# A vision tower on one Trainium2 core: attention's output products, its last division and one split, in another order

## The chip, the cores and the metric

The kernel runs on one core of one Trainium2 chip. Five engines work side by side, each through its own list of instructions in order: TensorE (PE, with its weight loads as PEld) multiplies and transposes, VectorE (DVE) and ScalarE (ACT) do elementwise work and read what TensorE left in PSUM, GpSimd (POOL) works in SBUF alone, and SyncE (SP) issues DMAs. They meet through semaphores only: an instruction that waits holds up everything behind it on its engine. The metric is the device time of one execution in microseconds (us), as the median of several.

## What is computed

One block of a vision transformer over 16 images of 37 positions (a class token and 36 patches), 592 rows of width 192. Cut to what matters:

```
h = patches of x, layer-normed over 3840 values, times W (3840x192), + b
h = concat(cls_tok, h)                                # 16 x 37 x 192
h = h + attention(layernorm(h))                       # 12 heads of 16, softmax with a bias by distance
h = h + ffn(layernorm(h))                             # shared expert (768) and 8 experts (192), two chosen

attention: q, k, v = x @ w_q.T + b_q, ...
           ctx  = softmax(q k / 4 + bias) @ v
           return ctx @ w_o.T + b_o
```

## The kernel before

The 592 rows lie in five tiles of 128 (tile 4 is part full), and the 16 images in eight pairs p of 74 rows. Large products in f16 are made of a high and a low part of each operand: ACT rounds a matrix to f16 (the high part) and DVE subtracts that from the original (the low part). No scheduler orders the work. Each engine's order is the order in which its calls are written, and semaphores named by the engine that raises them (p_, a_, v_, g_) tie them together.

The change lies in the stretch between the attention scores and the first feed-forward products. For its last pairs this happens:

- `scores(u)` on PE (L670, L680) makes the scores of two pairs, `differences(u)` on DVE (L1442, L1446) subtracts the row's largest, `exps(u)` on ACT (L1047) takes the exponential, `pt(p)` on PE (L695) transposes a pair, `weights_copy(p)` on ACT (L1072) copies it from PSUM, and `av(p)` on PE (L714) multiplies it with the values.
- `normalise(i)` on DVE (L1455, L1457) divides the contexts of pairs 2i and 2i+1 by their sums, `ct(p)` on PE (L729, L730) transposes them, and `ctx_high(i)` on ACT (L1066, eight small copies for the first two calls, four each) brings them back to SBUF as CA and CC.
- `wo(t)` on PE (L740, L742) is the output product of tile t. It waits until ACT has copied all pairs that reach into the tile: `ctx_high(0)` for tile 0, up to `ctx_high(3)` for tiles 3 and 4.
- `add_attention(t)` on DVE (L1478) adds the product to the residual stream in h2, L1374 and L1382 take mean and variance, `variances(k)` ends with L1385, `root(k)` on ACT (L985) takes the root, `rsqrt(k)` on DVE (L1334 to L1341) finishes it, `normed` (L1392) writes the normed tile, and `transposes(1, ...)` on PE (L600, L602) turns it. `copies` (L1003) on ACT comes between the two transposes of a tile. The tiles go in two groups: 0 to 2, then 3 and 4.
- `high_parts(1, ...)` on ACT (L996, L997) and `low_parts(1, ...)` on DVE (L1402) split the turned tiles, and `gu(i)` on PE (L828) multiplies them with the feed-forward weights. `gu(0)` and `gu(1)` run interleaved: twelve matmuls that need only the high parts, then eight that need the low parts. `gu(1)` waits for all five additions. Behind them come the transposes of tiles 3 and 4.
- The weights of the first third of the feed-forward are split in the same stretch: `ffn_high(0, q)` on ACT (L979) and `ffn_low(0, q)` on DVE (L1314), six steps each, wherever they are written in.

ACT changes its function table twice here, to Sqrt (L1088) and to Silu (L1095). PSUM has eight banks. SP's loads of the next weights wait for the last `av` and the last split (L386).

Of the kernel before, what the change touches and what calls it, by code (L numbers as in the profile page):

```python
# [20 lines left out]
ALU = mybir.AluOpType  # L21
# [3 lines left out]
P = 128  # L25
IMAGES, POSITIONS, D = 16, 37, 192
N = IMAGES * POSITIONS
# [70 lines left out]
def vit_kernel(nc, x_inner, x_ring, w_inner, w_ring, gb, consts, j_rev, ind, tok_b, cls, tab,  # L98
               aw_a, aw_b, aw_c, f_a, f_b, f_d, gate_rows, out):
    with ExitStack() as ctx:  # L100
# [176 lines left out]

        def attention_out(t):

            c0 = D * (0, 1, 0, 0, 1)[t]  # L280
            return PS[:, (3, 3, 4, 5, 5)[t], c0:c0 + D]

        def lane_cols(w, g):

# [141 lines left out]
        def _(pe):  # L426
# [167 lines left out]
            def transposes(n, banks, tiles):  # L594

                for t in tiles:
                    pe.wait_ge(S["v_hn"], TILES * n + t + 1)
                    oa = PS[:, banks[0], t * P:(t + 1) * P] if t < 3 else PS[:, banks[2], (t - 3) * P:(t - 2) * P]
                    ob = PS[:, banks[1], t * P:(t + 1) * P] if t < 3 else PS[:, banks[2], (t - 1) * P:t * P]
                    nc.tensor.transpose(oa, hn[:, t, 0:P], ident)  # L600
                    pe.wait_ge(S["a_dup"], TILES * n + t + 1)
                    nc.tensor.transpose(ob, hn[:, t, P:2 * P], ident).then_inc(S["p_t"], 1)  # L602
# [97 lines left out]
            def av(p):  # L700

                pe.wait_ge(S["a_pth"], p + 1)
                pe.wait_ge(d_vr[p // 4], 96)
                if p == 0:
                    pe.wait_ge(S["a_q"], 4)
                if p == 2:
                    pe.wait_ge(S["a_v"], 5)
                if p in (4, 6):
                    pe.wait_ge(S["v_cn"], p - 2)
                for r in range(LANES):  # L710
                    for bi in (0, 1):
                        q0, q1 = (0, 64) if bi == 0 else (64, QROWS)
                        c0 = (p % 2) * LANES * VW + r * VW
                        last = mm(PS[q0:q1, 1 + p // 2 % 2, c0:c0 + VW], PT[:, p, r, q0:q1],  # L714
                                  vv[:, 2 * p + bi, :, r * HV:(r + 1) * HV],
                                  start=(p % 2 == 0 and r == 0), stop=True, skip_group_check=True)
                last.then_inc(S["p_av"], 1)

            def ct(p):

                pe.wait_ge(S["v_cn"], p + 1)
                pe.wait_ge(S["g_one"], 2)
                if p == 0:
                    pe.wait_ge(S["v_sub"], 4)
                if p == 6:
                    pe.wait_ge(S["a_pth"], PAIRS)
                b = context_bank(p // 2)
                c0 = (p % 2) * 2 * QROWS
                nc.tensor.transpose(PS[:, b, c0:c0 + QROWS], cn[:, p, 0:P], ident[0:QROWS, 0:QROWS])  # L729
                nc.tensor.transpose(PS[:, b, c0 + QROWS:c0 + 2 * QROWS], cn[:, p, P:2 * P],  # L730
                                    ident[0:QROWS, 0:QROWS]).then_inc(S["p_ct"], 1)

            def wo(t):

                need = min(2 * (t + 1), PAIRS)
                pe.wait_ge(S["a_chi"], need)
                if t == 4:
                    pe.wait_ge(S["g_rows"], 2)
                tok = slice(t * P, (t + 1) * P)
                mm(attention_out(t), CA[:, tok], awst[:, 0, OC:OC + D], start=(t in (0, 2, 3)), stop=False,  # L740
                   skip_group_check=True)
                last = mm(attention_out(t), CC[:, tok], awst[0:CROWS, 2, OC:OC + D], start=False, stop=True,  # L742
                          skip_group_check=True)
                last.then_inc(S["p_wo"], 1)
# [34 lines left out]
                av(p)  # L779
            for p in (6, 7):  # L780
                pt(p)
            for p in range(4):
                ct(p)
            for p in (6, 7):
                av(p)
            for p in (4, 5):
                ct(p)
            for t in range(3):
                wo(t)
            for p in (6, 7):  # L790
                ct(p)
            wo(3)
            wo(4)
            transposes(1, (0, 1, 2), range(3))

            def router():

# [86 lines left out]
        def _(act):  # L884
# [86 lines left out]
            def ffn_high(p, q):  # L971

                if q == 0:
                    act.wait_ge(d_f[p], 48)
                Ah, _, Bw, Dh, _ = split(p)
                k, m = divmod(q, 2)
                W, st = (Ah, Bw, Dh)[k], stages(p)[k]
                part = slice(3 * m, 3 * m + 3) if k == 2 else slice(m, m + 1)
                A(W[:, part], st[:, part], ACT.Copy, scale=SW).then_inc(S["a_fw"], 1)  # L979

            def root(k):

                row, tiles, ready = NORMS[k]
                act.wait_ge(S["v_stat"], ready)
                A(small[:, row + 1, tiles[0]:tiles[-1] + 1], small[:, row, tiles[0]:tiles[-1] + 1],  # L985
                  ACT.Sqrt).then_inc(S["a_sqrt"], 1)
# [18 lines left out]
            def kq_high(f):  # L1005

                q, g, half = kq_product(f)
                cols = slice(half * HALF, (half + 1) * HALF)
                act.wait_ge(S["p_q" if q else "p_k"], 2 * half + g + 1)
                if f == 0:  # L1010
                    act.wait_ge(S["v_kk"], 2)
                if q:
                    A(Q32[:, g, cols], PS[:, kq_bank(f), 0:HALF], ACT.Copy, scale=QKS / XW).then_inc(S["a_q"], 1)
                else:
                    A(K32[:, 0, cols], PS[:, kq_bank(f), 0:HALF], ACT.Copy, scale=keven[:, :])
                    A(K32[:, 1, cols], PS[:, kq_bank(f), 0:HALF], ACT.Copy, scale=kodd[:, :]).then_inc(S["a_k"], 1)
# [36 lines left out]
            kq_high(6)  # L1053
            ffn_high(0, 1)
            kq_high(7)
            for t in (3, 4, 5):
                values_copy(t)
            exps(1)
            ffn_high(0, 2)

            def ctx_high(i):

                act.wait_ge(S["p_ct"], 2 * i + 2)
                for k, (C, rows) in enumerate(((CA, P), (CC, CROWS))):
                    for pr in (0, 1):
                        last = A(pair_cols(C, 2 * i + pr, rows), pair_queries(context_bank(i), pr, k, rows), ACT.Copy)  # L1066
                last.then_inc(S["a_chi"], 2)

            def weights_copy(p):

                act.wait_ge(S["p_pt"], p + 1)
                A(PT[:, p].rearrange("p r q -> p (r q)"), PS[0:BLOCK, (0, 7)[p % 2], 0:LANES * QROWS],  # L1072
                  ACT.Copy).then_inc(S["a_pth"], 1)
# [7 lines left out]
                weights_copy(p)  # L1081
            exps(3)
            ffn_high(0, 5)
            for p in (6, 7):
                weights_copy(p)
            ctx_high(0)
            ctx_high(1)
            A(small[:, 46, 0:1], one[:, :], ACT.Sqrt)  # L1088
            ctx_high(2)
            ctx_high(3)  # L1090
            root(3)
            copies(1, range(3))
            high_parts(1, (0, 1, 2), 0)
            root(4)
# [125 lines left out]
        def _(dve):  # L1220
# [86 lines left out]
            def ffn_low(p, q):  # L1307
# [6 lines left out]
                V.scalar_tensor_tensor(out=W[r0:P, part], in0=st[r0:P, part], scalar=SW, in1=hi[r0:P, part],  # L1314
                                       op0=ALU.mult, op1=ALU.subtract).then_inc(S["v_fw"], 1)

            for k in range(3):
                queries_keys_low(k)

# [47 lines left out]
            def residual(n, op, tiles):  # L1367

                src = (h1, h2)[n]
                for t in tiles:  # L1370
                    op(t).then_inc(S["v_h"], 1)
                for t in tiles:
                    dve.wait_ge(S["v_h"], TILES * n + t + 1)
                    V.bn_stats(bst[:, t, :], src[:, t, :]).then_inc(S["v_bn"], 1)  # L1374
                    bn[0] += 1
# [89 lines left out]
            ffn_low(0, 0)  # L1465
            differences(1)
            ffn_low(0, 1)
            differences(2)
            normalise(0)
            differences(3)  # L1470
            ffn_low(0, 2)
            normalise(1)
            normalise(2)
            for q in (3, 4):
                ffn_low(0, q)
            def add_attention(t):
                dve.wait_ge(S["p_wo"], (2, 2, 3, 5, 5)[t])
                return V.scalar_tensor_tensor(  # L1478
                    out=h2[:, t, :], in0=attention_out(t),
                    scalar=1.0, in1=h1[:, t, :], op0=ALU.mult, op1=ALU.add)  # L1480

            normalise(3)
            ffn_low(0, 5)
            residual(1, add_attention, (0, 1))
            residual(1, add_attention, (2,))
            variances(3)
            V.memset(ah[:, :, N:NPAD], 0.0)
            V.memset(al[:, :, N:NPAD], 0.0).then_inc(S["v_pad"], 1)
            rsqrt(3)
            dve.wait_ge(S["p_t"], TILES)  # L1490
            normed(1, range(3))
            residual(1, add_attention, (3, 4))
            variances(4)
            low_parts(1, (0, 1, 2), 0)
            rsqrt(4)
# [230 lines left out]
```

## Time and profile before

| what | us |
|---|---|
| median of 3 runs | 147.86 |
| lowest, highest | 147.77, 148.08 |
| the profiled execution, its own time | 147.91 |
| span of the profiled execution | 145.9 |
| PE busy in the span | 134.5 (92%) |
| DVE busy | 105.1 (72%) |
| ACT busy | 86.2 (59%) |
| POOL busy | 50.9 (35%) |
| share of PE in the chain that ended last | 64% |
| share of DVE, of ACT | 14%, 8% |

The profiled execution's own time is 2.0 us more than its span, which begins and ends with the engines' first and last work. Busy shares are averages over stages with different limits: in the stretch of this change three engines hand work to one another, so its rows are read one by one. "Idle before <-releaser" in brackets tells how long an engine stood before an instruction and what ended that. Rows of one engine overlap a little, since the next instruction starts while the last one drains.

### The profile page before, as it was taken

Reading aid. Unit: us, or ns where it says so; the run is one execution under the profiler, and the core shown is the slowest. Engines: PE = TensorE matmul, PEld = TensorE weight load, DVE = VectorE, ACT = ScalarE, POOL = GpSimd, SP = SyncE. Lnnn points to the kernel's source line nnn. Section 1 sums busy time; section 2 is a strip of 40 time slices with the busy share of each in tenths; the row PEclk is TensorE's granted clock in tenths of the full one; section 3 lists DMA queues with packets and bytes.
Section 4 is the critical chain, followed back from the end, with each engine's and each line's share of the span. In section 5 each row is a group of like instructions: output and inputs, shape, how many; then the busy total and the mean of one; then the engine's idle time right before and its main releaser. Section 6 shows DMA issues by size and latency. Waiting matters only on the chain.

```text
span 145.9 us, 3999 instructions
## 1 busy us (share of the span) xinstructions
PE 134.5 (92%) x1556; PEld 105.6 (72%) x1556; DVE 105.1 (72%) x268; ACT 86.2 (59%) x206; POOL 50.9 (35%) x72
## 2 busy tenths in 40 slices
PE   7768999999999999997899999998999999999991
PEld 2327679884676787985578788886887888888890
DVE  5499996899977978899876999838666224224453
ACT  0668769640488887883889756566553344344430
POOL 8149000500000000000025334785777577477330
PEclk9999999999999999999999999999999999999998
DMA  4999993078002233007993000368980000000003
GB/s 120 399 366 391 317 344 59 0 233 360 0 7 66 50 92 71 0 4 242 393 404 154 0 0 10 96 181 229 257 231 13 0 4 0 0 0 4 2 0 125
DMA packets 10580, 19.05 MB, mean 131 GB/s; under 512 B 2886, under 2 KB 6290, under 8 KB 10562
## 3 DMA queue, kind: packets, MB, share of 16 engines
q1 hardware_dynamic: 10218, 18.48, 39.3%
q10 hardware_dynamic: 344, 0.32, 0.8%
q8 instruction: 12, 0.20, 0.6%
q14 instruction: 6, 0.05, 0.1%
HBM read 17.84 MB, written 0.96 MB: 129 GB/s over the span
## 4 chain that ended last, share of the span: by engine, by line
PE 64%; DVE 14%; ACT 8%; DMA 5%; issue 4%; POOL 2%; SPq 1%; DVEq 0%; POOLq 0%
PE PS L828 25%; PE PS L858 12%; DMA xs<-in_x_inner_dram 5%; DVE we L1265 4%; PE PS L587 4%; PE PS L626 3%; PE PS L714 3%; PE PS L680 2%; PE PS L695 2%; DVE vhl L1579 2%; DVE xhl L1243 2%; POOL vhl L1200 2%; PE PS L670 1%; PE PS L506 1%; PE PS L569 1%
## 5 line engine op out<-in xcount | busy, mean ns | idle before, releaser
L1209 POOL TENSOR_TENSOR kq<-vhl,kq 128x296 f16<-128x296 f32 x35 | 28.2, 806 | 65.7 <-ACT kq L1116 65.7
L1579 DVE SCALAR_TENSOR_TENSOR vhl<-PS,vhl 128x296 f32<-128x296 f32 x36 | 16.8, 465 | 21.1 <-POOL vhl L1200 13.7
L1109 ACT ACTIVATE vhl<-PS 128x296 f32<-128x296 f32 x36 | 15.0, 415 | 25.6 <-PE PS L828 25.5
L1116 ACT ACTIVATE kq<-vhl 128x296 f16<-128x296 f32 x36 | 16.0, 445 | 4.2 <-DVE vhl L1579 4.2
L1200 POOL TENSOR_TENSOR vhl<-vhl,xs 128x296 f32<-128x296 f32 x14 | 12.5, 895 | 6.8 <-issue 6.0
L828 PE MATMUL PS<-XAh,slab 128*128 128x296 f16 x48 | 10.0, 290 | 0.7 <-DVE vhl L1579 0.7
L828 PE MATMUL PS<-XAh,piece 128*128 128x296 f16 x48 | 9.5, 289 | 1.0 <-ACT XAh L996 0.7
L1265 DVE SCALAR_TENSOR_TENSOR we<-slab,gbs,we 128x192 f32<-128x192 f32 x24 | 9.0, 445 | 1.6 <-ACT we L917 1.6
L828 PE MATMUL PS<-XAh,xsq 128*128 128x296 f16 x48 | 10.0, 289 | 0.0
L506 PE MATMUL PS<-whl,xhl 128*128 128x192 f16 (+1 forms) x40 | 9.9, 247 | 0.0
L508 PE MATMUL PS<-whl,xhl 128*128 128x192 f16 (+1 forms) x40 | 9.9, 246 | 0.0
L509 PE MATMUL PS<-whl,xhl 128*128 128x192 f16 (+1 forms) x40 | 9.8, 245 | 0.0
L858 PE MATMUL PS<-piece,kq 128*128 128x192 f16 x90 | 8.4, 246 | 0.0
L858 PE MATMUL PS<-slab,kq 128*128 128x192 f16 x90 | 8.4, 246 | 0.0
L858 PE MATMUL PS<-xsq,kq 128*128 128x192 f16 x90 | 8.2, 246 | 0.1
L858 PEld LDWEIGHTS PS<-xsq,kq 128*128 128x128 f16 x90 | 7.5, 98 | 0.5 <-issue 0.3
L858 PEld LDWEIGHTS PS<-slab,kq 128*128 128x128 f16 x90 | 7.6, 98 | 0.3
L858 PEld LDWEIGHTS PS<-piece,kq 128*128 128x128 f16 x90 | 7.6, 98 | 0.3
L492 PE MATMUL PS<-oneh 128*128 128x512 f16 x20 | 6.7, 498 | 1.0 <-DVE oneh L1223 1.0
L828 PE MATMUL PS<-XB,slab 128*128 128x296 f16 x24 | 6.9, 289 | 0.0
L828 PE MATMUL PS<-XAl,slab 128*128 128x296 f16 x24 | 6.9, 289 | 0.0
L828 PE MATMUL PS<-wring,slab 128*128 128x296 f16 x24 | 6.9, 289 | 0.0
(242 smaller groups left out, 363.9 us busy)
## 6 DMA issues: line engine op xcount, KB each, us to landing
slab<-in_w_inner_dram SPq DMA_DIRECT2D x3, 960.0 KB, 9.0
xs<-gate_rows_dram SPq DMA_DIRECT2D x8, 296.0 KB, 8.2
xs<-in_x_inner_dram SPq DMA_DIRECT2D x3, 592.0 KB, 10.0
stage<-in_f_a_dram SPq DMA_DIRECT2D x2, 768.0 KB, 4.9
stage<-in_f_b_dram SPq DMA_DIRECT2D x2, 768.0 KB, 6.4
stage<-gate_rows_dram SPq DMA_DIRECT2D x8, 148.0 KB, 7.3
stage<-in_f_d_dram SPq DMA_DIRECT2D x2, 576.0 KB, 7.1
xhl<-in_f_a_dram SPq DMA_DIRECT2D x1, 768.0 KB, 8.6
```

What stands on the lines that cost most here:

```text
L492: mm(PS[:, 1, :], oneh[:, :].to_broadcast([P, P]), oneh[:, :].to_broadcast([P, 512]), start=True, stop=True)
L506: mm(patch_out(t), xh[0:K, j, tok], wh[0:K, j, 0:D], start=(j == 0 and t in (0, 2, 3)), stop=False, skip_group_check=True)
L508: mm(patch_out(t), xl[0:K, j, tok], wh[0:K, j, 0:D], start=False, stop=False, skip_group_check=True)
L509: return mm(patch_out(t), xh[0:K, j, tok], wl[0:K, j, :], start=False, stop=(j == CHUNKS - 1), skip_group_check=True)
L828: last = mm(gate_up(i, m), w5[m][k], x5[k], start=(k == 0), stop=(k == 4))
L858: last = mm(o, a[:, f % ABUF, tok], w[:, f % PT_, :], start=(f in (0, ST) and t % 2 == 0 and k == 0), stop=(f in (ST - 1, FT - 1) and k == ...
L1109: A(silu[:, i % 2, :], gate_up(i, 0), ACT.Silu, scale=1.0 / XW).then_inc(S["a_silu"], 1)
L1116: A(ah[:, f % ABUF, half * HALF:(half + 1) * HALF], hf[:, i % 3, :], ACT.Copy).then_inc(S["a_ah"], 1)
L1200: G.tensor_tensor(sgate[:, i % 2, :], silu[:, i % 2, :], Gb[:, f_expert(f)[0], cols], ALU.mult).then_inc(S["g_sg"], 1)
L1209: G.tensor_tensor(al[:, f % ABUF, cols], hf[:, i % 3, :], ah[:, f % ABUF, cols], ALU.subtract).then_inc(S["g_al"], 1)
L1265: V.scalar_tensor_tensor(out=we[:, j, :], in0=slabv[:, s, j, :], scalar=gbs[:, 0, s * INNER + j:s * INNER + j + 1], in1=we[:, j, :], op0=A ...
L1579: V.scalar_tensor_tensor(out=hf[:, i % 3, :], in0=gate_up(i, 1), scalar=SH / XW, in1=src[:, i % 2, :], op0=ALU.mult, op1=ALU.mult).then_in ...
```

## The change

Four edits, all in the order of work or the place of results:

1. The product of tile 1 gets bank 6 and that of tile 4 bank 7, where they lay beside tiles 0 and 3 in banks 3 and 5. Each addition waits for its own product alone, and each tile is added and measured before the next.
2. PE makes the products of tiles 0, 1 and 2 before `av(6)` and `av(7)`, and turns tiles 0 to 2 between the products of tiles 3 and 4. ACT copies the contexts of pairs 0 to 5 between the weights of pair 6 and those of pair 7, and takes `root(3)` ahead of `ctx_high(3)`.
3. DVE makes the last division, `normalise(3)`, behind `variances(3)` and before `rsqrt(3)`. The two fills of the padding go behind the normed tiles.
4. DVE's third split step (64x768) becomes two of 64x384, ahead of `differences(2)` and behind `normalise(0)`. ACT's step for it moves up by four places, and DVE's other steps each move up by one place.

```diff
         def attention_out(t):
-            c0 = D * (0, 1, 0, 0, 1)[t]
-            return PS[:, (3, 3, 4, 5, 5)[t], c0:c0 + D]
+            return PS[:, (3, 6, 4, 5, 7)[t], 0:D]
...
-            for p in range(4):
-                ct(p)
-            for p in (6, 7):
-                av(p)
-            for p in (4, 5):
+            for p in range(6):
                 ct(p)
             for t in range(3):
                 wo(t)
             for p in (6, 7):
+                av(p)
+            for p in (6, 7):
                 ct(p)
             wo(3)
+            transposes(1, (0, 1, 2), range(3))
             wo(4)
-            transposes(1, (0, 1, 2), range(3))
...
+            ffn_high(0, 2)
             for t in (3, 4, 5):
                 values_copy(t)
             exps(1)
-            ffn_high(0, 2)
...
-            for p in (6, 7):
-                weights_copy(p)
-            ctx_high(0)
-            ctx_high(1)
+            weights_copy(6)
+            for i in range(3):
+                ctx_high(i)
+            weights_copy(7)
             A(small[:, 46, 0:1], one[:, :], ACT.Sqrt)
-            ctx_high(2)
+            root(3)
             ctx_high(3)
-            root(3)
...
+            def up_low_half(m, c):
+                _, _, Bw, _, _ = split(0)
+                part = (slice(64, P), m, slice(c * PC // 2, (c + 1) * PC // 2))
+                dve.wait_ge(S["a_fw"], 3 + m)
+                return V.scalar_tensor_tensor(out=Bw[part], in0=stages(0)[1][part], scalar=SW, in1=Bw[part],
+                                              op0=ALU.mult, op1=ALU.subtract)
...
             ffn_low(0, 1)
+            up_low_half(0, 0)
             differences(2)
             normalise(0)
+            up_low_half(0, 1).then_inc(S["v_fw"], 1)
             differences(3)
-            ffn_low(0, 2)
+            ffn_low(0, 3)
             normalise(1)
             normalise(2)
-            for q in (3, 4):
+            for q in (4, 5):
                 ffn_low(0, q)
             def add_attention(t):
-                dve.wait_ge(S["p_wo"], (2, 2, 3, 5, 5)[t])
+                dve.wait_ge(S["p_wo"], t + 1)
...
+            for t in range(3):
+                residual(1, add_attention, (t,))
+            variances(3)
             normalise(3)
-            ffn_low(0, 5)
-            residual(1, add_attention, (0, 1))
-            residual(1, add_attention, (2,))
-            variances(3)
-            V.memset(ah[:, :, N:NPAD], 0.0)
-            V.memset(al[:, :, N:NPAD], 0.0).then_inc(S["v_pad"], 1)
             rsqrt(3)
             dve.wait_ge(S["p_t"], TILES)
             normed(1, range(3))
-            residual(1, add_attention, (3, 4))
+            V.memset(ah[:, :, N:NPAD], 0.0)
+            V.memset(al[:, :, N:NPAD], 0.0).then_inc(S["v_pad"], 1)
+            for t in (3, 4):
+                residual(1, add_attention, (t,))
             variances(4)
```

In the kernel after, lines from 281 on have moved by one to six. On PE the end of attention stood so before, from the product of tile 2 (`we` holds the copied contexts, `xs` the divided ones, `hn` the normed tiles):

```order
L740 MATMUL PS<-awst,we 128x192 [waits a_chi]
L742 MATMUL PS<-awst,we 128x192
L729 MATMUL PS<-cst,xs 128x101 [waits a_pth,g_one,v_cn]
L730 MATMUL PS<-cst,xs 128x101
L729 MATMUL PS<-cst,xs 128x101 [waits g_one,v_cn]
L730 MATMUL PS<-cst,xs 128x101
L740 MATMUL PS<-awst,we 128x192 [waits a_chi]
L742 MATMUL PS<-awst,we 128x192
L740 MATMUL PS<-awst,we 128x192 [waits g_rows,a_chi]
L742 MATMUL PS<-awst,we 128x192
L600 MATMUL PS<-cst,hn 128x128 [waits v_hn]
```

The same end of attention on PE now, from the last transposes of the contexts (`av(6)` and `av(7)` stand right in front of those):

```order
L729 MATMUL PS<-cst,xs 128x101
L739 MATMUL PS<-awst,we 128x192 [waits a_chi]
L741 MATMUL PS<-awst,we 128x192
L599 MATMUL PS<-cst,hn 128x128 [waits v_hn]
L601 MATMUL PS<-cst,hn 128x128 [waits a_dup]
L599 MATMUL PS<-cst,hn 128x128 [waits v_hn]
L601 MATMUL PS<-cst,hn 128x128 [waits a_dup]
L599 MATMUL PS<-cst,hn 128x128 [waits v_hn]
L601 MATMUL PS<-cst,hn 128x128 [waits a_dup]
L739 MATMUL PS<-awst,we 128x192 [waits g_rows,a_chi]
L741 MATMUL PS<-awst,we 128x192
```

The first three tiles are turned behind one product instead of two, and the product of tile 4 comes after them. On DVE the last division stood so before, ahead of the additions (`rden`, `xs`: the division; `h`: the residual stream):

```order
L1455 RECIPROCAL rden<-PS 101x24 [waits p_av]
L1457 TENSOR_TENSOR xs<-PS,rden 101x2x192 [waits v_rd]
L1314 SCALAR_TENSOR_TENSOR piece<-stage,piece 128x576 [waits a_fw]
L1478 SCALAR_TENSOR_TENSOR h<-PS,h 128x192 [waits p_wo] x2
L1374 BN_STATS bst<-h 128x6 [waits v_h] x2
L1478 SCALAR_TENSOR_TENSOR h<-PS,h 128x192 [waits p_wo]
L1374 BN_STATS bst<-h 128x6 [waits v_h]
L1382 BN_AGGR mv<-bst 128x2 [waits v_bn]
L1382 BN_AGGR mv<-bst 128x2 x2
L1385 TENSOR_SCALAR small<-mv 128x3 [waits v_bn]
```

And on DVE now, from the addition of tile 2:

```order
L1484 SCALAR_TENSOR_TENSOR h<-PS,h 128x192 [waits p_wo]
L1378 BN_STATS bst<-h 128x6 [waits v_h]
L1386 BN_AGGR mv<-bst 128x2 [waits v_bn]
L1386 BN_AGGR mv<-bst 128x2 x2
L1389 TENSOR_SCALAR small<-mv 128x3 [waits v_bn]
L1459 RECIPROCAL rden<-PS 101x24 [waits p_av,v_stat]
L1461 TENSOR_TENSOR xs<-PS,rden 101x2x192 [waits v_rd]
L1338 RECIPROCAL small<-small 128x3 [waits a_sqrt]
L1343 TENSOR_TENSOR small<-small 128x3 [waits v_stat]
```

The division has gone behind the three additions and the variance, and it now waits for that variance (v_stat) as well as for `av(7)`.

## Rows read from the trace of the kernel before

**Rows 1.** The chain that ended last: start us, length us, what.

```profile
44.17 0.11 PE PS L600
...
70.82 2.68 PE PS L828 x20
```

**Rows 2.** Timeline of ACT, 61 to 67: start, length, engine, line, tiles, [idle before].

```profile
61.11 0.91 ACT L1072 ACTIVATE xhl<-PS 111x404 f32<-111x404 f32 x2 [0.65 <-PE PS L695]
61.90 1.09 ACT L1066 ACTIVATE we<-PS 128x74 f32<-128x74 f32 x8
63.01 1.28 ACT L1088 ACT_TABLE_LOAD   x1
...
64.41 0.58 ACT L1066 ACTIVATE we<-PS 128x74 f32<-128x74 f32 x4
66.35 0.60 ACT L1066 ACTIVATE we<-PS 128x74 f32<-128x74 f32 x4 [1.36 <-PE PS L730]
```

**Rows 3.** Timeline of PE, 61 to 66.

```profile
61.30 0.25 PE L729 MATMUL PS<-cst,xs 101*128 101x101 f32 x1
...
61.90 0.25 PE L730 MATMUL PS<-cst,xs 101*128 101x101 f32 x1
62.08 1.14 PE L714 MATMUL PS<-vhl,xhl 111*64 111x51 f32 x32
...
63.55 0.51 PE L740 MATMUL PS<-awst,we 128*128 128x192 f32 x2
...
64.23 0.49 PE L740 MATMUL PS<-awst,we 128*128 128x192 f32 x2
...
65.81 0.25 PE L729 MATMUL PS<-cst,xs 101*128 101x101 f32 x1
```

**Rows 4.** Timeline of DVE, 63 to 68.

```profile
63.27 0.31 DVE L1455 RECIPROCAL rden<-PS 101x24 f32<-101x24 f32 x1
63.68 0.56 DVE L1457 TENSOR_TENSOR xs<-PS,rden 101x384 f32<-101x384 f32 x1
...
65.08 0.62 DVE L1478 SCALAR_TENSOR_TENSOR h<-PS,h 128x192 f32<-128x192 f32 x2 [0.17 <-PE PS L742]
...
66.15 0.34 DVE L1478 SCALAR_TENSOR_TENSOR h<-PS,h 128x192 f32<-128x192 f32 x1
...
67.27 0.17 DVE L1385 TENSOR_SCALAR small<-mv 128x3 f32<-128x3 f32 x1
```

**Rows 5.** Timeline of all engines, 67 to 71: root, normed tiles, last transpose, high part.

```profile
67.71 0.18 DVE L1334 RECIPROCAL small<-small 128x3 f32<-128x3 f32 x1
...
68.51 0.96 DVE L1392 TENSOR_SCALAR hn<-h,mv,small 128x192 f32<-128x192 f32 x3
...
69.82 0.33 PE L602 MATMUL PS<-cst,hn 128*128 128x128 f32 x1
...
70.18 0.49 ACT L996 ACTIVATE XAh<-PS 128x384 f16<-128x384 f32 x1 [0.42 <-PE PS L602]
```

**Rows 6.** The same timeline, 71 to 74: tiles 3 and 4 on DVE and PE.

```profile
71.30 0.56 DVE L1402 SCALAR_TENSOR_TENSOR XAl<-PS,XAh 128x384 f16<-128x384 f32 x1 [0.28 <-ACT XB L997]
...
72.23 0.14 DVE L1334 RECIPROCAL small<-small 128x2 f32<-128x2 f32 x1
...
73.44 0.14 PEld L600 LDWEIGHTS PS<-cst,hn 128*128 128x128 f32 x1 [0.26 <-DVE hn L1392]
```

**Rows 7.** Timeline of DVE, 42 to 57: a split of half size, two idle times.

```profile
42.06 0.57 DVE L1304 SCALAR_TENSOR_TENSOR WB<-awst,WB 64x393 f16<-64x393 f32 x1
...
52.59 1.08 DVE L1442 TENSOR_REDUCE mx<-PS 101x24 f32<-101x888 f32 x1 [0.70 <-PE PS L680]
...
56.30 1.08 DVE L1442 TENSOR_REDUCE mx<-PS 101x24 f32<-101x888 f32 x1 [0.43 <-PE PS L680]
```

**Rows 8.** Timeline of all engines at 58.5 and of PE at 83.

```profile
58.53 0.95 DVE L1314 SCALAR_TENSOR_TENSOR piece<-stage,piece 64x768 f16<-64x768 f32 x1
...
82.96 0.43 PE L828 MATMUL PS<-XAh,piece 128*128 128x296 f16 x2 [0.33 <-DVE vhl L1579]
```

More of the change, by code:

```diff
@@ L739, in wo @@
                 tok = slice(t * P, (t + 1) * P)
-                mm(attention_out(t), CA[:, tok], awst[:, 0, OC:OC + D], start=(t in (0, 2, 3)), stop=False,
+                mm(attention_out(t), CA[:, tok], awst[:, 0, OC:OC + D], start=True, stop=False,
                    skip_group_check=True)
```

## The prediction, made before the change was timed

> **What bounds the kernel now.** I read the chain that ended last first, since it tells which stage sets the end. From 57 to 74 us it runs through this stretch without a break, and from 70.82 on it is TensorE alone with the twenty matmuls of the first two feed-forward halves, 0.134 us each [rows 1]. So what counts is when TensorE gets to those, and when it gets past the transposes of tiles 3 and 4 behind them. Then I read the engines' timelines from 61 us, where each hand-over shows. ScalarE copies the last two pairs' weights, pays a Sqrt table of 1.28 us in the middle of the contexts, and waits 1.36 us for TensorE before the last context [rows 2]. TensorE makes the last two value products early, from 62.08 to 63.22, and then the output products, 0.68 us each where nothing waits [rows 3]. VectorE divides at once, at 63.27, and is ready for the additions at 65.08 [rows 4]. The root and the normed tiles follow at 67.71 and 68.51, the last of the six transposes at 69.82, the high part at 70.18 [rows 5]. Tiles 3 and 4 are turned at 73.44, after 0.26 us of waiting for VectorE [rows 6]. All the work behind that hangs on what it hands over.
>
> **The split in two halves: nothing.** A whole step takes 0.95 us [rows 8]. A half of 64x384 is bounded by half of that, 0.48, and by a step of 64x393, 0.57 [rows 7]. I take 0.55, being nearer to the row of that width. The first half falls into 0.70 us of idle time. The second falls into 0.43 us, so it may delay the last score maxima by 0.05 to 0.14 [rows 7]. ScalarE, whose exponential would wait for that, is busy with weight copies then, which covers it. The two halves take 0.95 us of VectorE out of the later stretch. ScalarE's cast moves ahead of the value copies and delays those by about 0.3; their readers come over 1 us later. If that cover were gone, 0.14 us at most would be lost on VectorE's side and 0.3 on ScalarE's.
>
> **Products ahead of the last value products: earlier additions.** The transposes start at 61.30 and follow at 0.086, each 0.25 long [rows 3], so the first context is ready at 61.81 and ScalarE, now one weight copy shorter, starts on it at 61.84. Four copies take 0.60 alone, 0.48 in a row [rows 2]: the first context ends at 62.44, the third at 63.40. From the end of a context's copies at 64.99 [rows 2] to TensorE's next work behind the product it released, 65.81 [rows 3], are 0.82. So product 1 starts at 62.44 + 0.82 = 63.26, product 2 at 63.94, and TensorE is free for the value products at 64.62. From a product's start (64.23 [rows 3]) to its addition (65.08 [rows 4]) are 0.85: the addition of tile 2 starts at 63.94 + 0.85 = 64.79 instead of 66.15. From there to the end of the variance's chain are 1.12 (66.15 to 67.27 [rows 4]): 65.91 instead of 67.27, a gain of 1.36. The own banks cost nothing and let tile 0's addition go ahead of product 1; tile 2's sets the end, so this gives nothing either.
>
> **The Sqrt table: covered.** The seventh weight copy ends at 63.8, the table of 1.28 [rows 2] at 65.1, the root starts at 66.1.
> Here the Trainium skill speaks against the change (ScalarE: Activation LUTs, What ACT_TABLE_LOAD costs): a switch is about 1283 ns and a drain of 1380 ns behind it. The trace agrees with the first and shows no drain, since 64.41 follows on 63.01 + 1.28 with a dummy activation between [rows 2]. With the drain the Sqrt switch would still fit before the root, but the later Silu switch, which now starts 0.7 later, would hold the first silu by a further 1.4 us.
>
> **The last division: 1 us behind what the output needs.** The value products end at 64.62 + 1.14 = 65.76. The division stands behind the variance: 65.91, 0.17 long [rows 4], and 0.10 to the next step as between the division's own two, so 66.18. Its second part starts 0.41 later and takes 0.56 [rows 4]: 67.15, where it was 64.24. VectorE's own chain loses little by this: the root ran meanwhile, and its reciprocal starts at 67.1 instead of 67.71, the normed tiles at 67.9 instead of 68.51 [rows 5]. But TensorE's order decides. Four transposes take 0.57 out of a wait (three steps of 0.086, 0.25, 0.06 to get going), from 67.21 to 67.78. The last context's copies start at 67.81 and end at 68.41 [rows 2]. Product 3 waits for them and the transposes of the normed tiles stand behind it: 68.41 + 0.82 = 69.23. With all tiles ready these go at 0.11 [rows 1], the last at 69.78 instead of 69.82 [rows 5]. So 1.36 us of gain have shrunk to 0.04, and the first feed-forward matmul starts at 70.78 instead of 70.82.
>
> **Product 4 behind the transposes: the loss.** It starts at 69.89 and its addition at 69.89 + 0.85 = 70.74. VectorE has been done with everything else since 69.0 and waits. From this addition to the end of the variance I take 1.02 (1.12 less about 0.1 for two tiles in place of three): 71.76. The low parts stand behind that, + 0.27 as above: 72.03 instead of 71.30 [rows 6]. From there on the order is as before: 0.93 to the reciprocal [rows 6], 0.80 to the normed tiles [rows 5], 0.41 to TensorE: 74.17 instead of 73.44. TensorE will have finished all twenty matmuls by then but for a wait for the low parts, which cover 70.78 to 73.46. **The sum is + 0.73 us at TensorE's transposes of tiles 3 and 4.** Root 4 and the Silu table behind it move by as much, so nothing catches up there. SP's loads of the next weights wait for the value products and start up to 0.8 later; they have no reader for some 8 us, so that costs nothing.
>
> The profiled execution took 147.91, so + 0.73 is 148.64. The median of the runs stands 0.05 below that execution: **148.6**.
>
> **Rivals.** *Partly taken up (no change).* If the division started when the value products end, at 65.8, the tail would be 0.4 shorter, + 0.35; and a later wait of 0.33 [rows 8] could take the rest, if it isn't moved along. For it: VectorE's hand-overs are my least sure terms. Against: the row at 82.96 is a wait for VectorE, whose chain starts from the moved work. It gives 147.9. *Faster.* The addition of tile 4 would have to be early enough for both the low parts (by 72.2) and the normed tiles (by 73.4) to be ready when TensorE asks. Then the 0.26 of waiting [rows 6] and up to 0.2 at the front are won: 147.4. It decides at a last context ready by 67.6, against 68.41 above. For it: the variance is 1.36 earlier, and each of the seven hand-overs is only an estimate. Against: the value products alone, at 65.76, leave 0.4 of the 0.8. *More than forecast.* TensorE stands idle for 1.4 us from 65.8 and 0.6 from 67.8. Before, its granted clock stayed at 2.4 GHz through waits of up to 0.7. A fall to 1.2 GHz would double the twenty matmuls' 2.68 us [rows 1]: some 151.
>
> **How the numbers follow.** Forecast (148.2 to 149.0) 0.67; no change 0.16; faster 0.11; more than forecast 0.06. A measurement of this kernel can tell about 0.2%, 0.3 us, from no change. Faster by more than that has 0.11, slower by more 0.67 + 0.06 = 0.73. The range has to reach to the no-change case: 147.8 to 149.0 leaves out some 0.17.
>
> **What would show it.** In the profile after: the addition of tile 2 near 64.8 and its variance near 65.9; the division near 66.2, right behind the variance; a wait of TensorE of about 1.4 us before the last context's transposes, and one of 0.6 before product 3; the transposes of the normed tiles behind product 3 without a wait for VectorE; a wait of VectorE of over 1 us before the addition of tile 4; the low parts near 72.0 and TensorE's transposes of tiles 3 and 4 near 74.2; and from there on every step 0.7 later than before. It is wrong if the division runs before the variance, if product 3 is done before the normed tiles are, or if waits behind 80 us shrink by what was lost.

## The result, and the profile after the change

The changed kernel took 149.18 us (median of 4 executions, 148.43 to 150.37) against 147.81 before: a ratio of 1.0087, 95% interval 1.0055 to 1.0119. It is slower, as forecast, but by 1.37 us instead of 0.7, and the median lies above the range. Here and below a ratio leaves out executions over 1.5% above the fastest of their kernel and the medians leave out none, so that a ratio stands below the quotient of its medians where long executions are many.

The four times can't be understood without TensorE's mean granted clock: 148.43 (0.998), 148.57 (0.999), 149.78 (0.988) and 150.37 (0.984). Two of them kept the full clock nearly throughout, two didn't. The profiled one is of the first kind, 148.43 against 147.91 before, + 0.52. I take that first, and then what the other kind adds.

PE, from the last value products on, in the timeline after the change (start, length, engine, line, tiles, [idle before <-releaser]; lines stand one to six off those of before):

```profile
64.55 1.13 PE L713 MATMUL PS<-vhl,xhl 111*64 111x51 f32 x32
67.03 0.30 PE L728 MATMUL PS<-cst,xs 101*128 101x101 f32 x1 [1.34 <-DVE xs L1461]
...
68.28 0.59 PE L739 MATMUL PS<-awst,we 128*128 128x192 f32 x2 [0.69 <-ACT we L1063]
...
69.04 0.27 PE L599 MATMUL PS<-cst,hn 128*128 128x128 f32 x1
...
69.69 0.49 PE L739 MATMUL PS<-awst,we 128*128 128x192 f32 x2
...
70.53 0.66 PE L825 MATMUL PS<-XAh,piece 128*128 128x296 f16 x4
...
72.44 0.42 PE L825 MATMUL PS<-XAl,piece 128*128 128x296 f16 x2 [0.24 <-DVE XAl L1406]
...
73.97 0.33 PE L599 MATMUL PS<-cst,hn 128*128 128x128 f32 x1
...
83.48 0.43 PE L825 MATMUL PS<-XAh,piece 128*128 128x296 f16 x2 [0.33 <-DVE vhl L1585]
```

These answer to [rows 3], [rows 5] and [rows 6]. One wait is new, 1.34 us for the last division. The 0.69 for the last context was there before, at 67.00:

```profile
67.00 0.59 PE L740 MATMUL PS<-awst,we 128*128 128x192 f32 x2 [0.69 <-ACT we L1066]
```

It now comes 1.28 us later, and starts 0.56 us behind the end of the new one. The waits of 0.37 and 0.67 us that the kernel before had behind its product 4, for the normed tiles and for the high part, are gone in exchange. The transposes of tiles 0 to 2 (69.04) stand right behind product 3, waiting for nothing. Those of tiles 3 and 4 start at 73.97 instead of 73.44, and the wait at 83.48 is 0.33 long as it was at 82.96 [rows 8]: the loss is carried on unchanged.

DVE in the same timeline, which answers to [rows 4] and [rows 6]:

```profile
64.68 0.34 DVE L1484 SCALAR_TENSOR_TENSOR h<-PS,h 128x192 f32<-128x192 f32 x1
...
65.80 0.17 DVE L1389 TENSOR_SCALAR small<-mv 128x3 f32<-128x3 f32 x1
66.00 0.31 DVE L1459 RECIPROCAL rden<-PS 101x24 f32<-101x24 f32 x1
66.41 0.56 DVE L1461 TENSOR_TENSOR xs<-PS,rden 101x384 f32<-101x384 f32 x1
66.89 0.17 DVE L1338 RECIPROCAL small<-small 128x3 f32<-128x3 f32 x1
...
67.68 0.96 DVE L1396 TENSOR_SCALAR hn<-h,mv,small 128x192 f32<-128x192 f32 x3
...
70.55 0.36 DVE L1484 SCALAR_TENSOR_TENSOR h<-PS,h 128x192 f32<-128x192 f32 x1 [0.56 <-PE PS L741]
...
71.82 0.56 DVE L1406 SCALAR_TENSOR_TENSOR XAl<-PS,XAh 128x384 f16<-128x384 f32 x1
...
73.53 0.67 DVE L1396 TENSOR_SCALAR hn<-h,mv,small 128x192 f32<-128x192 f32 x2
```

The variance is 1.47 us earlier than in [rows 4] (65.80 for 67.27), the normed tiles 0.83 earlier than in [rows 5] (67.68 for 68.51), and yet the low parts come 0.52 later than in [rows 6] (71.82 for 71.30).

### The profile page after: what moved, and what is told of

Read it like the earlier page. It is cut to its first block, busy times and chain, and to the rows that moved or that the text cites. A ratio compares the mean times of both kernels' runs of the same rounds, so it can differ in the third digit from the quotient of the medians.

```text
span 146.4 us, 4001 instructions
## 1 busy us (share of the span) xinstructions
PE 134.9 (92%) x1556; PEld 105.6 (72%) x1556; DVE 105.6 (72%) x269; ACT 85.9 (59%) x206; POOL 50.9 (35%) x72
## 4 chain that ended last, share of the span: by engine, by line
PE 62%; DVE 16%; ACT 8%; DMA 5%; issue 4%; POOL 2%; SPq 1%; DVEq 0%; POOLq 0%
PE PS L825 23%; PE PS L855 12%; DMA xs<-in_x_inner_dram 5%; DVE we L1261 4%; PE PS L586 4%; PE PS L625 3%; PE PS L679 2%; PE PS L713 2%; PE PS L694 2%; DVE vhl L1585 2%; DVE xhl L1239 2%; POOL vhl L1196 2%; PE PS L669 1%; PE PS L505 1%; PE PS L568 1%
```

## The experiments

The theory from the prediction: the division behind the variance makes the last context late, product 3 and the transposes queue behind it, and product 4 behind those makes the tail late. New beside it: in some executions TensorE's granted clock falls in this stretch. The rivals: the spread has nothing to do with the stretch; the banks or the halves cost the time. All ran with 8 to 12 executions, beside 23 to 35 of the kernel before, whose medians were 147.96, 147.97 and 147.98. They ran in three groups, each on a chip of its own. The first had the changed kernel again, the long wait filled, product 4 moved alone and the early division; the second the short wait filled, the halves, the whole split and the banks; the third product 4 moved with the long wait filled, and the early division again. So the changed kernel ran beside the first group only. Three single executions took over 300 us (341.55, 341.51, and 466.74 of the kernel before); they stand in the medians and not in the counts. Without them the early division has 147.57 instead of 147.62, and the whole split 147.84 instead of 147.87.

**The changed kernel again.**

> The changed kernel once more, to see how its times are spread. Four executions gave 148.43, 148.57, 149.78 and 150.37 us, with a mean granted clock of 0.998, 0.999, 0.988 and 0.984. Theory A (the clock falls in some executions): again two groups, one at 148.4 to 148.7 with a clock of 0.998 or more, one 1 to 2 us longer with a clock under 0.99, some half of them. Theory B (chance of the session, as in any kernel): nearly all at 148.4 to 148.7, or the kernel before beside it is spread as well.

Measured: 149.85 us, ratio 1.0099 (1.0067 to 1.0132). Two of eight executions took 148.52 and 148.93 at a clock of 0.998 and more, six 149.64 to 150.85 at 0.986 to 0.988. With the four above that is 4 against 8. The quotient of the medians is 1.013; the ratio leaves out the longest execution. The lowest clock among the 31 executions of the kernel before beside it was 0.996. It isn't quite proof against a fall either: of all 89 executions of the kernel before in the three groups one took 149.41 us at a clock of 0.988. Theory A holds, and this profiled execution is of the long kind. Its stretches, with TensorE's granted clock in the column PEclk (1.00 is 2.4 GHz, 0.50 is 1.2 GHz):

```profile
core 0: us, PE busy (x) PEld busy (x) DVE busy (x) ACT busy (x) POOL busy (x), PEclk, DMA share, GB/s
66.00:68.00 2.00, 0.66 (x16) 0.54 (x13) 1.76 (x9) 0.20 (x1) 0.00 (x0) 1.00 0.09 11
68.00:70.00 2.00, 1.31 (x8) 1.10 (x7) 1.46 (x8) 1.25 (x7) 0.00 (x0) 0.88 0.91 296
70.00:72.00 2.00, 2.00 (x10) 1.93 (x9) 0.72 (x2) 0.40 (x2) 0.00 (x0) 0.50 0.98 361
72.00:74.00 2.00, 2.00 (x13) 1.51 (x13) 1.02 (x5) 0.47 (x2) 0.00 (x0) 0.77 1.05 405
```

TensorE was busy for 0.66 and 1.31 of two 2 us stretches, and then its clock was at the lower level throughout the next. The execution above, which stands 0.77 us earlier, was much the same there at the full clock:

```profile
66.00:68.00 2.00, 0.56 (x4) 0.37 (x4) 1.76 (x8) 0.57 (x5) 0.00 (x0) 1.00 0.43 65
68.00:70.00 2.00, 1.72 (x12) 1.70 (x13) 1.52 (x7) 0.99 (x6) 0.00 (x0) 1.00 0.95 341
```

So what TensorE did doesn't settle by itself whether the clock falls. PE's timeline of the long execution:

```profile
65.32 1.14 PE L713 MATMUL PS<-vhl,xhl 111*64 111x51 f32 x32
67.79 0.31 PE L728 MATMUL PS<-cst,xs 101*128 101x101 f32 x1 [1.34 <-DVE xs L1461]
...
69.05 0.59 PE L739 MATMUL PS<-awst,we 128*128 128x192 f32 x2 [0.69 <-ACT we L1063]
69.48 0.80 PE L741 MATMUL PS<-awst,we 97*128 97x192 f32 x2
70.07 0.42 PE L599 MATMUL PS<-cst,hn 128*128 128x128 f32 x1
...
71.35 0.85 PE L739 MATMUL PS<-awst,we 128*128 128x192 f32 x2
71.99 0.85 PE L741 MATMUL PS<-awst,we 97*128 97x192 f32 x2
72.63 0.81 PE L825 MATMUL PS<-XAh,piece 128*128 128x296 f16 x4
...
76.30 0.33 PE L599 MATMUL PS<-cst,hn 128*128 128x128 f32 x1
```

Both waits are as long as above. The clock falls at 69.5, within product 3 (the first pair of its matmuls takes 0.59, the second 0.80), and is back at 72.9, within the first feed-forward matmuls. Product 4 takes 1.28 us from start to the next work, against 2 x 0.33 for its two pairs of matmuls at the full clock (69.69 to 70.02 above). This execution stands 0.77 later than the one above before the stretch begins (65.32 for 64.55), so at the transposes of tiles 3 and 4 the lower clock has cost 76.30 - 73.97 - 0.77 = 1.56 us.

**The long wait filled.** The edit:

```diff
             for p in (6, 7):
                 av(p)
+            keep_warm(1, 6)
             for p in (6, 7):
                 ct(p)
```

> The changed kernel with six dummy matmuls of 512 columns (0.22 us each) on TensorE between the last value product and the last context's transposes, where it waits 1.34 us. They lie inside the wait, so the order of the rest is untouched. Theory A (TensorE's idle time before the last context is what makes the clock fall): all executions at 148.4 to 148.7, clock 0.998 or more. Theory A2 (the other idle times do it as well): long executions are fewer but there. Theory B (the spread has nothing to do with this wait): the same spread as the changed kernel's, median 149.2.

Measured: 148.57 us, ratio 1.0031 (1.0014 to 1.0049). None of twelve executions fell under a clock of 0.995, and the longest took 148.93. PE's timeline:

```profile
65.60 1.47 PE L586 MATMUL PS<-WAh 128*128 128x512 f16 x6
67.00 0.31 PE L728 MATMUL PS<-cst,xs 101*128 101x101 f32 x1
...
73.94 0.33 PE L599 MATMUL PS<-cst,hn 128*128 128x128 f32 x1
```

The work behind starts when it did (73.94 for 73.97). So this separates the two losses: 148.57 - 147.96 = 0.6 us from the order of the work, and the rest from the clock. Six matmuls without use win back 1.3 us of the median of the run beside it, in which the clock was low in six of eight executions.

**The short wait filled.** `keep_warm(1, 3)` stands ahead of `wo(3)` instead, and the long wait stays idle.

> The changed kernel with three dummy matmuls of 512 columns on TensorE in the other wait, the 0.69 us between the last context's transposes and product 3; the 1.34 us before those transposes stay idle. If any idle time of the stretch counts alike, filling half as much makes long executions rarer but not gone (between 1 and 6 in 12, against 8 in 12 of the changed kernel and none in 12 with the longer wait filled). If only the one longest wait counts, they are as frequent as in the changed kernel. Undisturbed executions at 148.4 to 148.7 either way.

Measured: 148.57 us, ratio 1.0036 (1.0014 to 1.0057), none of twelve executions under 0.995. I had expected fewer falls, not none.

```profile
67.20 0.31 PE L728 MATMUL PS<-cst,xs 101*128 101x101 f32 x1 [1.34 <-DVE xs L1462]
...
67.61 0.81 PE L586 MATMUL PS<-WAh 128*128 128x512 f16 x3
68.45 0.59 PE L739 MATMUL PS<-awst,we 128*128 128x192 f32 x2
```

The wait of 1.34 us is still there. Neither wait alone brought the clock down in a dozen executions; the two together went with a low clock in eight of twelve. The changed kernel didn't run in this group, so that this count is compared with one from other chips; for the long wait the two ran side by side.

**Product 4 ahead of the transposes**, first alone, then with the long wait filled as above:

```diff
             wo(3)
-            transposes(1, (0, 1, 2), range(3))
             wo(4)
+            transposes(1, (0, 1, 2), range(3))
```

> The changed kernel with the product of tile 4 back ahead of the transposes of tiles 0 to 2. If the late context alone sets the tail: the transposes start some 0.65 later, near 69.7, tile 4's addition some 0.6 earlier, and the transposes of tiles 3 and 4 start within 0.2 of where they are after the change (73.97): the undisturbed executions at 148.3 to 148.6. If the product's place behind the transposes is the loss, as the prediction has it: the transposes of tiles 3 and 4 come 0.5 earlier, 147.9.

> The changed kernel with product 4 ahead of the transposes of tiles 0 to 2, and the first wait filled with the six dummy matmuls, so that the clock can't blur the comparison with e1_warm (148.57, 12 executions). If the late context alone sets the tail, the undisturbed e3_wo4_first (148.40) was no accident: 148.3 to 148.5, all executions at a clock of 0.995 or more; the transposes of tiles 0 to 2 start some 0.65 later than in e1_warm (69.01) and those of tiles 3 and 4 within 0.25 of 73.94. If the product's place was the loss: 147.9 to 148.1.

Measured: 149.45 us for the first, six executions at 148.16 to 148.93 (median 148.40) and six at 149.97 to 151.32 with a clock of 0.972 to 0.987. The profiled one took 150.89:

```profile
68.35 1.01 PE L739 MATMUL PS<-awst,we 128*128 128x192 f32 x2 [0.69 <-ACT we L1063]
```

Here the clock fell earlier, at 67.9 and within the wait of 0.69 us, and it was low until 74.8, into the feed-forward matmuls. That execution is 2.5 us over the undisturbed median. The second: 148.22 us, ratio 1.0017 (0.9997 to 1.0038), 0.35 below e1_warm, which is between the two outcomes that I had written down. One of its executions had a mean clock of 0.988, at 148.78; it is the profiled one, and its clock fell at 6 to 8 us, under the loads at the start, where TensorE had waited 2.17 us for a DMA, and stood at 1.00 throughout this stretch. So a mean clock of 0.988 alone doesn't tell where the clock fell. Its PE timeline:

```profile
68.93 0.59 PE L739 MATMUL PS<-awst,we 128*128 128x192 f32 x2 [0.69 <-ACT we L1064]
...
70.34 0.27 PE L599 MATMUL PS<-cst,hn 128*128 128x128 f32 x1
...
71.83 0.66 PE L826 MATMUL PS<-XAh,piece 128*128 128x296 f16 x4 [0.67 <-ACT XAh L994]
...
74.35 0.27 PE L599 MATMUL PS<-cst,hn 128*128 128x128 f32 x1
```

Counted from product 3, the transposes of tiles 3 and 4 come at + 5.42 here and at 73.97 - 68.28 = + 5.69 in the changed kernel: 0.27 earlier, though the feed-forward starts 0.65 later. So the product's place was worth 0.35 of the 0.6 by the medians with the wait filled, 0.27 by the trace, and 0.15 by the undisturbed executions of the first run (148.40 against 148.55 of the changed kernel's four, inside what I had written down for the late context alone). What is left goes with the late product 3: the feed-forward can't start before the transposes behind it.

**The last division early.** With banks and halves as changed, but both value products ahead of the output products, the division as soon as they are done, and ScalarE's three contexts ahead of the Sqrt table. Against the changed kernel:

```diff
             for p in range(6):
                 ct(p)
+            for p in (6, 7):
+                av(p)
             for t in range(3):
                 wo(t)
             for p in (6, 7):
-                av(p)
-            for p in (6, 7):
                 ct(p)
             wo(3)
-            transposes(1, (0, 1, 2), range(3))
             wo(4)
+            transposes(1, (0, 1, 2), range(3))
...
             weights_copy(6)
+            weights_copy(7)
             for i in range(3):
                 ctx_high(i)
-            weights_copy(7)
             A(small[:, 46, 0:1], one[:, :], ACT.Sqrt)
-            root(3)
             ctx_high(3)
+            root(3)
...
+            normalise(3)
             for t in range(3):
                 residual(1, add_attention, (t,))
             variances(3)
-            normalise(3)
+            V.memset(ah[:, :, N:NPAD], 0.0)
+            V.memset(al[:, :, N:NPAD], 0.0).then_inc(S["v_pad"], 1)
             rsqrt(3)
             dve.wait_ge(S["p_t"], TILES)
             normed(1, range(3))
-            V.memset(ah[:, :, N:NPAD], 0.0)
-            V.memset(al[:, :, N:NPAD], 0.0).then_inc(S["v_pad"], 1)
-            for t in (3, 4):
-                residual(1, add_attention, (t,))
+            residual(1, add_attention, (3, 4))
```

> Banks of their own, all five transposed pairs up to 5 and both last value products early, the division as soon as they are done, ScalarE's three contexts ahead of the Sqrt table, the output products behind, the product of tile 4 ahead of the transposes, split in two halves. If the late last division is the cause of the loss: additions of tile 2 near 65.6, variance near 66.7, normed tiles near 67.9, and everything behind 0.3 to 0.5 earlier than before: 147.4 (147.2 to 147.6), faster than both. If the own banks or the halves cost something by themselves: 147.8 or more. Clock 0.998 or more in all executions, since no wait of TensorE is longer than before.

> e4_early_ctx once more, to narrow the interval: its first eleven undisturbed executions had a median of 147.57 against 147.96 of the kernel before beside it. If that gain is real: 147.4 to 147.7 again, 0.3 to 0.5 below the kernel before, no execution at a clock under 0.99. If it was chance: 147.8 or more.

Measured: 147.62 us, ratio 0.9975 (0.9955 to 0.9994), and again 147.50, ratio 0.9958 (0.9939 to 0.9976): 0.3 to 0.5 us faster than the kernel before, and the first of the two over 2 us faster than the changed one beside it. No execution fell under a clock of 0.995. From the timeline of all engines:

```profile
63.47 0.31 DVE L1459 RECIPROCAL rden<-PS 101x24 f32<-101x24 f32 x1 [0.73 <-PE PS L713]
...
66.61 0.59 PE L739 MATMUL PS<-awst,we 128*128 128x192 f32 x2 [0.69 <-ACT we L1063]
...
66.79 0.17 DVE L1389 TENSOR_SCALAR small<-mv 128x3 f32<-128x3 f32 x1
...
68.46 0.33 PE L599 MATMUL PS<-cst,hn 128*128 128x128 f32 x1 [0.28 <-DVE hn L1396]
...
72.85 0.27 PE L599 MATMUL PS<-cst,hn 128*128 128x128 f32 x1
```

The variance is a microsecond later than in the changed kernel (66.79 for 65.80), and the kernel is faster: product 3 starts at 66.61 instead of 68.28, so that products 3 and 4 are done when the normed tiles come, and TensorE waits for VectorE again. The transposes of tiles 3 and 4 come at 72.85. This kernel takes back several things at once: product 4 is ahead of the transposes again (0.15 to 0.35 us, as above) and tiles 3 and 4 are added in a pair again. Of the 0.95 us to the changed kernel with its long wait filled (148.57) that leaves some 0.4 to 0.8, an estimate with up to 0.2 for the pairs as measured below, to the early division and what follows from it. The division wasn't moved alone.

**The halves alone, and the halves taken out of the faster kernel.**

> The kernel before with edit 4 alone: the split in two halves in earlier gaps, the other steps one place up. By the prediction it is worth nothing by itself: 147.8 to 148.1, within 0.1% of the kernel before beside it, with the additions of tiles 0 to 2 where they were since they wait for TensorE. The rival, that it lets the last division and the additions start earlier, would give 0.2 us or more.

> The kernel with the early last division (e4) with edit 4 undone. There the division waits 0.73 us for TensorE with the split moved away; with the whole split step of 0.95 us back in front of it, the division should start 0.2 to 0.3 later and the end come later by as much: 147.7 to 147.9 against 147.5. If the halves are worth nothing here either: 147.5.

Measured: 147.77 us, ratio 0.9988 (0.9967 to 1.0008), no difference that this can tell; and for the faster kernel without the halves 147.87, ratio 0.9991 (0.9976 to 1.0005), against 147.50 and 147.62 with them in the other two groups. Without them the division starts at 64.10, right behind the split steps, instead of after a wait of 0.73:

```profile
64.10 0.30 DVE L1459 RECIPROCAL rden<-PS 101x24 f32<-101x24 f32 x1
...
71.43 0.56 DVE L1406 SCALAR_TENSOR_TENSOR XAl<-PS,XAh 128x384 f16<-128x384 f32 x1 [0.28 <-ACT XB L994]
```

The execution above with its 63.47 stands 0.35 earlier from the context transposes on. The second profile with the halves is level with this one (context transposes at 61.48 and 61.50) and has the division at 63.80, 0.3 earlier. So the halves are worth some 0.3 us in that order, by the traces and the medians; the intervals of the ratios overlap or touch.

The second line shows something that I hadn't looked for. In all three kernels without the halves (before, the banks alone, this one) the low parts start 0.44 to 0.46 us behind the start of the variance's last step, with 0.28 idle. With the halves they start 0.20 or 0.21 behind it, in all traces but that of product 4 moved alone, where the high part came late; with the halves alone that is 71.12 instead of 71.30 [rows 6]. The profile names ScalarE's last high part for the wait, but in the kernel before that ends at 71.05, 0.25 ahead of the low parts. Why the halves take this wait away is not shown. The variance's last step in the kernel before, for the 0.46:

```profile
70.84 0.17 DVE L1385 TENSOR_SCALAR small<-mv 128x2 f32<-128x2 f32 x1
```

**The banks and the tile-by-tile order alone.**

> The kernel before with edit 1 alone: products 1 and 4 in banks of their own, each tile added and measured before the next. Tile 2's addition is set by product 2, so the variance stays where it was: within 0.1 us of the kernel before beside it (147.8 to 148.1). If the one-at-a-time order costs VectorE 0.1 us per tile, tiles 3 and 4, which are not covered by TensorE, come 0.1 to 0.2 later: up to 148.1.

Measured: 148.23 us, ratio 1.0014 (0.9997 to 1.0032); eleven executions at 148.06 to 148.35, one at 149.20 with a clock of 0.988. The interval just touches no change. DVE's timeline shows where 0.2 us go (this execution stands 0.07 earlier than that of before, the context transposes at 61.23):

```profile
67.19 0.17 DVE L1384 TENSOR_SCALAR small<-mv 128x3 f32<-128x3 f32 x1
...
69.31 0.35 DVE L1477 SCALAR_TENSOR_TENSOR h<-PS,h 128x192 f32<-128x192 f32 x1
69.69 0.36 DVE L1373 BATCH_NORM_STATS2 bst<-h 128x6 f32<-128x192 f32 x1
69.97 0.34 DVE L1477 SCALAR_TENSOR_TENSOR h<-PS,h 128x192 f32<-128x192 f32 x1
...
71.46 0.56 DVE L1401 SCALAR_TENSOR_TENSOR XAl<-PS,XAh 128x384 f16<-128x384 f32 x1 [0.28 <-DVE small L1384]
```

For tiles 0 to 2 nothing is lost (67.19 for 67.27 [rows 4]). For tiles 3 and 4 a measurement that needs the addition in front of it starts 0.38 us behind it (69.31 to 69.69), and one instruction that needs nothing 0.28 (69.69 to 69.97). Additions and measurements in pairs hide that; one by one they don't, and the low parts start at 71.46 instead of 71.30 [rows 6]. The Trainium skill (VectorE: DVE Perf Modes, The DRAIN you can't avoid) tells of eight copies that took the same time with a semaphore behind each and with one behind the last only. Here every addition and every measurement raises a semaphore, and what costs 0.1 us is to wait for that of the instruction right in front, at a length of 0.35 us; no run here shows it for longer ones.

## Why the prediction was wrong

By its own steps, for an execution whose clock holds, it was right nearly throughout. The trace after stands 0.10 us earlier than that of before by 61 us (the context transposes start at 61.20, not 61.30), so 0.10 of each difference below is this head start.

| step | forecast | measured |
|---|---|---|
| addition of tile 2 | 64.79 | 64.68 |
| end of the variance's chain | 65.91 | 65.80 |
| division | 66.18 | 66.00 |
| last context's transposes | 67.21 | 67.03 |
| transposes of tiles 0 to 2 | 69.23 | 69.04 |
| first feed-forward matmul | 70.78 | 70.53 |
| addition of tile 4 | 70.74 | 70.55 |
| low parts | 72.03 | 71.82 |
| transposes of tiles 3 and 4 | 74.17 | 73.97 |
| profiled execution | 148.64 | 148.43 |

- **The step that failed is the clock's term, which the sum put at nothing.** The two waits of TensorE entered the sum as time only, and every matmul behind them at the full clock. The fall stood in the rival "more than forecast" with a chance of 0.06 and a price of 2.7 us, and the range ended at 149.0 without it. Measured: 8 of 12 executions ran at a mean clock of 0.984 to 0.988 and took 149.64 to 150.85 instead of 148.43 to 148.93, and with the long wait filled none of twelve did. The argument for the low chance, that the clock had held through waits of up to 0.7, spoke of a stretch without a wait of 1.34 followed by one of 0.69; for the two together there was no row, and I should have put the case inside the range. It also left out the waits at the start of the same trace: 1.59 us before 11.35, at a granted clock of 1.00, so the longest single wait was a bad measure either way. The price was too high for this kernel because I laid the lower clock on the twenty feed-forward matmuls, while it lay on product 3, the transposes and product 4, which is 1.56 us in the long execution profiled. With product 4 moved ahead it did reach those matmuls, and cost 2.5.
- **The division behind the variance:** right. It started 0.20 behind the variance, and the kernel that takes it forward again, with product 4 and the pairs, turned the loss into a gain.
- **Product 4 behind the transposes, "the loss":** half right. With the product in front 0.15 to 0.35 of 0.6 us came back; the late product 3 holds the tail either way. I had counted its delay as neutral since the front lost nothing.
- **The banks cost nothing:** right up to the first variance, but I did not price the tile-by-tile order for tiles 3 and 4, worth 0.2 us by the rows. It was inside the sum all the same, since the sum went by single steps.
- **The halves are worth nothing:** on the kernel before no difference could be told. They are worth some 0.3 us in an order where the division is what VectorE's work holds up. In this change they weren't tested alone; the low parts' wait of 0.28 us is gone in it, and that the sum had so was luck: it put the low parts 0.27 behind the variance, where the rows of before have 0.46 (70.84 to 71.30).
- **The tables:** right. After the change the Sqrt table starts at 63.73 and the next activation at 65.03, so there is no drain in this trace either, as I had read from [rows 2].
- **No catching up later:** right. The transposes of tiles 3 and 4 come 0.53 us later (73.97 for 73.44), and 0.52 are there at the end. The stretch itself loses 0.63, of which the head start of 0.10 is off.

## What to carry to other kernels

An early result is worth something only if what the next engine does first depends on it: here the variance came 1.5 us earlier, but the transposes that wanted it were queued behind a product whose operand had been put behind that very variance. When an order opens a new wait on TensorE, price it twice, once as time and once as clock, and look at the spread and the mean clock of several executions, since one profile shows one execution only. A few dummy matmuls in such a wait are a cheap test, and here a cheap cure.

## What the runs showed of the hardware

In 8 of 12 executions of one and the same program TensorE's mean granted clock was 0.984 to 0.988. In the one of them that was profiled it fell from 2.4 to 1.2 GHz at 69.5 us, behind waits of 1.34 and 0.69 us, and was back at 72.9. The longest single wait doesn't decide it: the same execution had waits of 1.44 and 1.65 us under the loads at its start, at a granted clock of 1.00 throughout. Filling 1.3 us of the first wait or 0.65 us of the second was followed by no fall in 24 executions. The Trainium skill (TensorE: Matmul & The Clock Gate, HAM oscillation) tells of a clock brought down again and again by TensorE's waits for DMAs. The trace agrees that idle time brings it down, and the waits here, 1.34 and 0.69 us for VectorE and ScalarE, are shorter than those that the page has. Why four of twelve executions with the same two waits kept the clock is not shown, and where between the two fillings and the unfilled kernel the line lies was not tried.
